# An AdaLN block with attention and a routed feed-forward: the near slots move in front of the last three dense tiles

## The reference, cut to what matters

```python
h = _layernorm(x) * (1 + ca) + sa
x = x + ga * attention(h)              # 16 heads of 128, causal, 1024 tokens
h = _layernorm(x) * (1 + cb) + sb
logits = h @ gate_w.T                  # 8 experts
top_vals, top_idx = top_k(logits, 2)
w = softmax(top_vals)
y = einsum('td,eod->teo', h, expert_w) + expert_b
x = x + gb * sum(take(y, top_idx) * w)
```

## Time and profile before

| | |
|---|---|
| times of 3 executions | 896.4, 898.64, 899.07 us |
| the profiled execution | 900.1 us, its span 898.2 us |
| PE busy | 867.4 us (97%) |
| DVE busy | 743.5 us (83%) |
| ACT busy | 541.2 us (60%) |
| POOL busy | 325.6 us (36%) |
| DMA | 43.08 MB, mean 48 GB/s |

### The profile page before, as it was taken

How to read it: one execution, slowest core, us unless ns; L and a number is a source line. 1 busy time by engine, 2 the same in 40 slices (tenths; PEclk the granted TensorE clock), 3 DMA queues, 4 the chain that set the end, 5 groups by cost and what they waited for, 6 DMA issues and landing times.

```text
span 898.2 us, 16979 instructions
## 1 busy us (share of the span) xinstructions
PE 867.4 (97%) x5399; PEld 771.4 (86%) x5399; DVE 743.5 (83%) x1688; ACT 541.2 (60%) x1247; POOL 325.6 (36%) x398
## 2 busy tenths in 40 slices
PE   6999999999999999999999999999999999999985
PEld 5778888888888888888888889988998888889884
DVE  6687888888888888878878888888889989887666
ACT  4477666666666666664566666666666656664351
POOL 4454222222222222231534444444422224576644
PEclk9999999999999999999999999999999999999998
DMA  7000620000000000200000000000000000352563
GB/s 246 7 12 12 229 65 14 12 12 12 12 12 12 12 12 12 96 17 7 1 24 13 14 12 13 13 12 14 12 13 13 13 12 30 130 171 77 195 210 112
DMA packets 36649, 43.08 MB, mean 48 GB/s; under 512 B 3060, under 2 KB 33814, under 8 KB 36502
## 3 DMA queue, kind: packets, MB, share of 16 engines
q1 hardware_dynamic: 34216, 35.94, 12.4%
q0 software_dynamic: 2304, 6.29, 2.2%
q10 hardware_dynamic: 64, 0.02, 0.0%
HBM read 32.02 MB, written 15.20 MB: 53 GB/s over the span
## 4 chain that ended last, share of the span: by engine, by line
PE 89%; DVE 5%; ACT 2%; DMA 1%; issue 1%; POOL 0%; SPq 0%; DVEq 0%; ACTq 0%
PE ps_t L1063 13%; PE ps_s L952 9%; PE ps_s L956 9%; PE ps_s L953 9%; PE ps_o L944 7%; PE ps_o L948 7%; PE ps_o L945 7%; PE ps_m L952 3%; PE ps_m L956 3%; PE ps_m L953 3%; PE ps_m L944 3%; PE ps_m L948 3%; PE ps_m L945 3%; PE ps_o L1073 1%; PE ps_t L1152 1%
## 5 line engine op out<-in xcount | busy, mean ns | idle before, releaser
L1423 ACT ACTIVATE pt_hi<-ps_t 128x512 fp32r<-128x512 f32 (+2 forms) x320 | 170.9, 534 | 124.6 <-PE ps_t L1063 124.2
L1473 ACT ACTIVATE probs<-ps_s,neg_max 128x128 f32<-128x128 f32 (+7 forms) x256 | 189.9, 742 | 79.5 <-DVE neg_max L1857 76.5
L1866 DVE TENSOR_TENSOR pt_lo<-ps_t,pt_hi 128x512 fp32r<-128x512 f32 (+2 forms) x320 | 192.1, 601 | 13.0 <-ACT pt_hi L1423 9.1
L1857 DVE TENSOR_REDUCE neg_max<-ps_s 128x1 f32<-128x128 f32 (+7 forms) x256 | 192.3, 751 | 3.7
L703 POOL TENSOR_TENSOR q_lo<-raw,q_hi 128x512 fp32r<-128x512 f32 x60 | 77.4, 1290 | 312.5 <-ACT q_hi L1423 312.4
L1063 PE MATMUL ps_t<-ident,probs 128*128 128x128 f32 x1152 | 188.6, 272 | 0.9 <-DVE pt_lo L1866 0.9
L1063 PEld LDWEIGHTS ps_t<-ident,probs 128*128 128x128 f32 x1152 | 141.8, 141 | 20.7 <-DVE pt_lo L1866 4.9
L952 PE MATMUL ps_s<-k_hi,q_hi 128*128 128x512 f32 (+2 forms) x354 | 148.5, 420 | 2.4 <-ACT probs L1473 2.4
L1904 DVE SCALAR_TENSOR_TENSOR acc<-ps_m,rsum,acc 128x256 f32<-128x256 f32 x256 | 111.3, 476 | 16.3 <-PE ps_m L956 15.7
L956 PE MATMUL ps_s<-k_hi,q_lo 128*128 128x512 f32 (+2 forms) x354 | 123.3, 348 | 0.0
L1851 DVE TENSOR_TENSOR ps_s<-ps_s,mask 128x128 f32<-128x128 f32 x256 | 75.4, 295 | 57.0 <-PE ps_s L956 49.5
(11 more groups left out here) (311 smaller groups left out, 1719.4 us busy)
## 6 DMA issues: line engine op xcount, KB each, us to landing
slot_out_dram<-y_slot SPq DMA_DIRECT2D x38, 128.0 KB, 1.7
wq_raw<-in_L_attn_wq_dram SPq DMA_DIRECT2D x32, 128.0 KB, 2.3
wo_raw<-in_L_attn_wo_dram SPq DMA_DIRECT2D x32, 128.0 KB, 2.0
wkv_raw<-in_L_attn_wkv_dram SPq DMA_DIRECT2D x2, 1024.0 KB, 6.3
acc<-in_L_attn_x_dram SPq DMA_DIRECT2D x2, 1024.0 KB, 15.4
we_raw<-in_L_ffn_expert_w_dram SPq DMA_DIRECT2D x1, 2048.0 KB, 8.4
slot_rows<-slot_rows_dram SPq DMA_DIRECT2D x2, 1024.0 KB, 7.6
slot_rows_dram<-in_L_attn_x_dram SPq DMA_DIRECT2D x1, 1920.0 KB, 16.4
```

The costliest lines, as they stand in the source:

```text
L1423: return nc.scalar.activation(dst, src, ACT.Copy, scale=scale)
L1473: nc.scalar.activation(probs[par][:, prob_offset(i):prob_offset(i) + w], ps_s[:, i % 2, col:col + w], ACT.Exp, bias=neg_max[:, par, i:i + ...
L1857: nc.vector.tensor_reduce(neg_max[:, par, i:i + 1], ps_s[:, i % 2, col:col + w], AXIS_X, ALU.max, negate=True).then_inc(max_set, 1)
L1866: nc.vector.tensor_tensor(pt_lo[:, q % PT, lo:CH], ps_t[:, q % 2, lo:CH], pt_hi[:, q % PT, lo:CH].bitcast(F32), ALU.subtract).then_inc(pt_ ...
```

## The change

The near slots stand directly behind dense tile 0; dense tiles 1 to 3 follow them. The transposes of the first two near slots, which lay behind the third and fourth expert pair of tile 1, now lie behind those of tile 0. Joins 0 to 5 lie among the near slots, joins 6 to 10 inside tiles 1 to 3, join 11 behind the last finish. SP issues the second and third load of near rows when the first has landed. The gates of the late rows, the reading of their logits and the work on them are one slot later each, and the low plane of slot 0 is made one step earlier on DVE.

```diff
-JOIN_AT = {1: 1, 3: 2, 6: 3, 9: 4, 12: 5}
+JOIN_AT = {2: 0, 5: 1, 7: 2, 9: 3, 11: 4, 13: 5}
+DENSE_EARLY = 0
@@ banks
-            return kv_bank(s % 2) if s < SLOTS else kv_bank(2 + (s - SLOTS) % 2)
+            return kv_bank(s % 2)
-            return kv_bank((e2 + (2 if d < 2 else 0)) % 4)
+            return kv_bank((e2 + 2) % 4)
@@ SP
             for i, (lo, hi) in enumerate(((0, 3), (3, 9), (9, SLOTS1))):
+                if i == 1:
+                    sp.wait_ge(slots1_in[0], 16)
                 sp.dma_start(slot_rows1[:, lo:hi, :], slot1_v[:, lo:hi, :]).then_inc(slots1_in[i], 16)
...
@@ PE
                 if s in (SLOTS, SLOTS + 1):
-                    pe.wait_ge(*((first_mixed, 4) if s == SLOTS else (mixed, LATER_MIXES + 2)))
+                    pe.wait_ge(mixed, LATER_MIXES)
-                elif d == 2:
-                    pe.wait_ge(*((mixed, LATER_MIXES + 4 + 2 * e2) if e2 < 2 else (slot_out, ALL_SLOTS)))
+                elif d == 1 and e2 in (0, 2):
+                    pe.wait_ge(*((first_mixed, 2) if e2 == 0 else (slot_out, ALL_SLOTS)))
-            gate_after = {4: 0, 5: 1, 7: 2, 9: 3, 12: 4, 14: 5, 16: 6, 18: 7}
+            gate_after = {4: 0, 5: 1, 7: 2, 9: 3, 13: 4, 15: 5, 17: 6, 19: 7}
             for d in range(HALF):
-                if d == 2:
-                    for s in range(SLOTS, ALL_SLOTS):
-                        if s + 2 < ALL_SLOTS:
-                            turn_slot(s + 2)
-                        slot_product(s, near_e[s - SLOTS])
                 for e2 in range(EXPERTS // 2):
+                    if d == 1 and e2 == DENSE_EARLY:
+                        for s in range(SLOTS, ALL_SLOTS):
+                            if s + 2 < ALL_SLOTS:
+                                turn_slot(s + 2)
+                            slot_product(s, near_e[s - SLOTS])
                     experts(d, e2)
-                    if d == 1 and e2 == 0:
+                    if d == 0 and e2 == 1:
                         pe.wait_ge(n_place_set, 1)
                         near_e.extend(chosen(n_expert_u, SLOTS1))
-                    if d == 1 and e2 >= 2:
+                    if d == 0 and e2 >= 2:
                         turn_slot(SLOTS + e2 - 2)
@@ DVE, behind the slots of batch 0
+            mix(0, {})
+            slot_lower(SLOTS)
+            slot_lower(SLOTS + 1)
+            finish(0)
+            hidden2_lo(2)
+            for s in range(SLOTS, ALL_SLOTS):
+                if s + 2 < ALL_SLOTS:
+                    slot_lower(s + 2)
+                if s - SLOTS in JOIN_AT:
+                    join(JOIN_AT[s - SLOTS])
+            mix(1, {5: 6})
+            hidden2_lo(3)
+            finish(1)
+            mix(2, {3: 7, 7: 8})
+            mix(3, {3: 9, 5: 10})
+            finish(3)
+            join(JOINS - 1)
```

More of the change, by code:

```diff
@@ L586, in _ @@
             store_mixed(0)
-            store_mixed(1)
-            store_joined(0)
             for s in range(SLOTS1):
@@ L592, in _ @@
                     store_joined(JOIN_AT[s - 1])
-            for j in range(NT - 2, NT + 2):
+            store_joined(6)
+            store_mixed(1)
+            for j in range(7, JOINS - 1):
                 store_joined(j)
+            store_mixed(2)
             store_mixed(3)
-            store_joined(NT + 2)
-            store_joined(NT + 3)
-            store_mixed(2)
+            store_joined(JOINS - 1)
             for i in range(2):
@@ L1703, in _ @@
                     hidden2_hi(s - 16)
-                if s == 19:
+                if s == 20:
                     read_logits(late, 2 * HALF)
-                if s == 21:
+                if s == 22:
                     gap_exponential(late)
             slot_finish(SLOTS - 1)
[L1709 to L1714, removed]
-                            slot_finish(s - 1)
-                        if s - SLOTS in JOIN_AT:
-                            weigh_first(JOIN_AT[s - SLOTS])
-                    slot_finish(ALL_SLOTS - 1)
-                mix_first(d)
-                if d == 1:
-                    slot_upper(SLOTS)
-                    slot_upper(SLOTS + 1)
-                if d + 2 < HALF:
-                    hidden2_hi(d + 2)
-                if d == 1:
-                    weigh_first(0)
-                if d == 2:
-                    weigh_first(NT - 2)
-                    weigh_first(NT - 1)
-            for j in range(NT, JOINS):
+            mix_first(0)
+            slot_upper(SLOTS)
+            slot_upper(SLOTS + 1)
+            hidden2_hi(2)
+            for s in range(SLOTS, ALL_SLOTS):
+                if s + 2 < ALL_SLOTS:
+                    slot_upper(s + 2)
+                if s > SLOTS:
+                    slot_finish(s - 1)
+                if s - SLOTS in JOIN_AT:
+                    weigh_first(JOIN_AT[s - SLOTS])
+            slot_finish(ALL_SLOTS - 1)
+            mix_first(1)
+            weigh_first(6)
+            hidden2_hi(3)
+            mix_first(2)
+            weigh_first(7)
+            weigh_first(8)
+            mix_first(3)
+            for j in range(NT + 1, JOINS):
                 weigh_first(j)
@@ L1957, in frame @@
                     if q == 11 and not nxt:
+                        if b + 1 == B:
+                            slot_lower(0)
                         add_projection(n, par, b, 0, 1)
@@ L2305, in finish, with mix @@
                                         ALU.add).then_inc(yout_set[par], 1)
-            def mix(d, joins):
+            def mix(d, joins, some=range(2, EXPERTS)):
                 par = d % 2
-                for e in range(2, EXPERTS):
+                for e in some:
                     if e % 2 == 0:
@@ L2321, in mix @@
                         join(joins[e])
-                    if d == 1 and e in (5, 6):
-                        slot_lower(SLOTS + e - 5)
             def join(j):
@@ L2341, in _ @@
             n = B * HEADS - 1
-            slot_lower(0)
             slot_lower(1)
```

25 lines of the change are left out of this document (5 added, 20 removed).

## The result

Median of 11 executions: 901.63 us (900.32 to 904.03) against 899.07 us (896.4 to 901.33) of the kernel before in 11 executions beside it. The forecast was 0.7 us more (899.3 us), in a range of 895.3 to 902.8 that held the time.

A forecast was written before the change was run, and what follows sets the result against it. PE stalls and low clock in the near slots, then DVE at the end, were taken as the bound. Last matmul 890.8 plus 8.1 gives 898.9 against 898.2; 0.7 on the 898.64 median gives 899.3 us, range 895.3 to 902.8.

The forecast's parts named there:

- mixes and low plane on DVE: Behind the fourth pair of tile 0: DVE mixes two halves (0.87 us), then makes the first near slot's plane (0.42).
- first two slots: Behind the stall: 2.5 us of DVE planes and tile 0's finish cover these slots; the third slot starts at 857.0.
- the gates: Late-row gates one slot later: PE's 0.66 us wait for DVE goes; 0.3 us taken, between 0 and 0.7.
- The wait for the load: Before the first near slot's transposes: PE stands 4.4 us, until the near rows land at 849.4.
- The load alone: First near-row load, issued without the other two: little won, landing in 3.4 us, between 2.5 and 3.9.
- The clock: Behind the stall: 1.2 GHz for two transposes and the fourth pair; full clock 1.8 us less, slow slots 1 more.
- The slots: The thirteen slots left: 13.9 us, plus 0.7 (0 to 2.5) for slack eaten at joins and a late store.
- The end: Behind the last matmul: 8.1 us in place of 10.1, 2.0 us won; bounds 6.6 and 8.7.
- A: Faster rival at the first-load wait: the stall costs only its length, 2.4 GHz kept; 897.0 us; chance 0.20.
- B: Slower rival at the fourth near slot: the second load comes late, PE stops again; 901.8 us; chance 0.18.
- C: Rival in slots and load: DVE falls behind, the load gains nothing alone; 1.2 us more, 900.5; chance 0.12.
- The signs: Idle 4.4 us, clock 0.50, second stop over 1 us, last matmul 2 to 3 us later, end some 8 behind.

The follow-up runs named there:

- gates_only: The kernel before with only the gates of the late rows and their ACT and DVE steps one slot later; no difference that can be told.
- unsplit: The changed kernel without SP's wait between the first and second load of near rows; the same time as the changed kernel within its interval.
- warm: The changed kernel with 19 unread matmuls filling PE's wait for the first load; ratio 1.0001 to the kernel before, 2.0 us back from the change.
- early_rows: The changed kernel, its first near-row load taken from batch 0's buffer without waiting for the scatter; 1.9 us faster than the changed kernel.
- two_pairs: The changed kernel with near slots behind tile 1's second pair, their first two transposes behind its first and second; 897.29 us, ratio 0.9982 to the kernel before.
- warm_join4: The changed kernel with 19 filler matmuls in the wait and four joined buffers in place of two; ratio 0.0005 below that of warm.
- join4: The changed kernel with four buffers for joined tiles in place of two; ratio 0.0006 (0.5 us) lower than the change, not distinguishable from nothing.

## Why the prediction was right, and by which steps

The number was right by a range that is wide for this change, and in part because errors of opposite sign met. Counted from the issue of the first load, which the forecast had at 846.04 and the trace has at 845.72:

```
step                                    forecast   trace    difference
landing of the first load               3.4        3.69     +0.3
transposes and fourth pair              3.6        3.69     +0.1
mixes and low plane on DVE              1.5        1.28     -0.2
first two slots                         2.5        3.75     +1.3
thirteen slots                          14.6       15.31    +0.7
dense tiles 1 to 3                      19.2       19.06    -0.1
from there to the end                   8.1        7.20     -0.9
sum                                     52.9       54.0     +1.1
```

From the same point to the end the kernel before takes 51.86 us, so the forecast had 1.0 us more here and 0.3 us less ahead of it, from the gates; that is its 0.7. The trace has 2.1 us more here. Ahead of it nothing was won: gates_only shows the wait moved, and that the load is issued 0.6 us earlier than before is no gain of the edit, since this execution lacks the low clock at 29 to 34 us. Of the traces that have that stretch, the four of changed kernels issue the load at 846.7 to 846.9, and the kernel before at 846.34.

**The wait for the load: right.** 4.51 us for 4.4, released by the load.

**The load alone: right.** I took little gain from it and put it at 3.4 us between 2.5 and 3.9; it took 3.69, and 3.6 with the others behind it. The low bound of 2.5, worked out from a bandwidth, was reached in no trace (3.4 to 4.0).

**The clock: right in kind, too small in size.** The granted clock fell to 0.50 and the pair took what was forecast. I let it recover at the pair's end and kept "low for the first two slots too, 1 us more" as the upper bound. That bound is what happened in the profiled execution, where the clock was back just before 858; in unsplit's trace it returned sooner, and the same stretch took 1.5 us less. In the place of this cost the forecast had DVE's queue: finish and planes were to delay the third slot to 857.0. In the trace DVE waited for PE's transposes by way of ACT instead, 0.81 us at 857.45. This is the mis-sized term, +1.3 us in this execution, and warm put the clock's whole price at 2.7 us in its trace and 2.0 us in time, where the forecast held 1.8. The mean clocks, 0.9915 over the changed kernel's executions and 0.9935 over those of the kernel before, point the same way, but they count stretches in which nothing is lost and cannot be turned into the price of this one.

The Trainium skill (TensorE: Matmul & The Clock Gate, section "HAM oscillation — how this bites in real kernels") says that a matmul burst behind a long DMA wait starts cold. The changed kernel and early_rows agree (clock 0.50 behind 4.51 and 2.45 us); behind the shorter waits for loads in two_pairs (1.08 and 1.85 us) the clock is 1.00; and warm shows the reverse: with the wait filled the clock stays at 1.00.

**The slots: half right.** PE stood for 0.76 us here, for 0.7 forecast, but by another cause: five joins were cheap, as assumed, and one was held 1.0 us by its buffer, not by a slowly eaten slack. The late store that I took over from the kernel before did not occur in this trace; unsplit and warm have it. The 0.7 us more are in the slots themselves: PE was busy for 14.55 us in place of 13.9, and from transposes to transposes a slot took 1.13 us on average, without the stall, and not 1.10.

**The end: right in sign, 0.9 us too cautious.** DVE ended 4.9 us past the last matmul and not 5.4, and the last store took 2.3 and not 2.7. Of the 5.4, 0.2 were a slip: 8.4 less 3.2 is 5.2. The slowed DVE step beside POOL's finish is there (0.84 at 887.50) and lies ahead of the last matmul, as the forecast had it.

**Rivals.** A fell: the clock did drop. B did not occur, but its mechanism is real and showed itself in four kernels in which PE came to the fourth slot sooner (0.19 us in warm, 0.22 in warm_join4, 1.85 in two_pairs, 2.45 in early_rows). C was right about the load and wrong about DVE.

**The signs.** The wait, the clock behind it and an end more than 7 us behind the last matmul came as said. The second stop was 0.87 us and not over a microsecond, and the last matmul ended at 892.5, 4.4 us later than 888.1 and not 2 to 3.

The forecast was 1.4 us below the measured difference (0.7 against 2.1, interval 1.2 to 3.0). 1.1 of this are the terms above, with the clock as the largest and the end as a credit against it; the other 0.3 are the gates.

## What to carry to other kernels

Before work that waits for a transfer is moved forward, compare when its data can land with when the engine would come for it, and put as much independent work of the same engine in front of it as the difference: here two expert pairs (with the loads issued at once) turned +0.23% into -0.32%. A stall of PE is priced at its length plus what the low clock takes behind it, until the clock is seen to be back and not until the next step ends. And once such a stall goes, look at the next load and the buffers of the stores: the next waits in these traces stand there. Before two traces are compared, look at the clock over the whole of each: here a low stretch 800 us ahead of the change goes with a shift of about a microsecond in everything behind it.

## What the runs showed of the hardware

- **How long PE stood, and what the clock did.** In the traces from 840 us on, stalls of 1.04 to 1.85 us (eight kernels) left the granted clock at 1.00; stalls of 2.19 (gates_only), 2.22 (before), 2.45 (early_rows) and 4.3 to 4.5 us (after, unsplit, join4) came with 0.50. These are single traces: the executions of two_pairs, with its 1.85 us, have mean clocks from 0.999 (896.4 us) down to 0.992 (901.95 us), and what lowered the clock in the slow ones is not shown.
- **The clock falls inside a long stall, or just behind one of 2.2 us.** In before PE was back at work at 858.75 and the clock fell at about 859.2; in gates_only it was 857.46 and about 857.8. In the longer stalls it fell while PE stood. In after it was 0.85 over the microsecond from 847 and 0.50 from 848, while the rows landed at 849.4; in join4, with a stall as long, it fell only at 849.4, and in unsplit already at 846.5. Where it fell earlier it also came back earlier: at 853.2 in unsplit, 857.9 in after and 859.6 in join4. Why it stays low for about 7 us in one and 10 in the others is open.
- **The spread between executions goes with the clock, and not only in this stretch.** In every kernel the time falls with the mean clock of its executions (correlation -0.44 to -0.99), by 0.5 to 0.8 us for 0.001 in most of them. Six of the twelve profiled executions have a clock of 0.50 for a while between 29 and 34 us, with PE at work: in before it follows sixteen matmuls of 2 columns each and a stall of 0.50 us at 27 us, and matmuls of 512 columns start 0.43 us apart in it and 0.23 us apart elsewhere. Where it is there, the first load is issued about a microsecond later.
- **The clock column does not hold at the start of a trace.** At 8.13 us in before, behind a stall of 5.54 us, those sixteen matmuls take 3.55 us against 1.95 at 27 us, with 1.00 in both windows.
- **Loads in one queue.** The first load of 384 KB landed in 3.4 to 4.0 us in all traces, alone or with 1.5 MB behind it. A load of 768 KB took 4.83 (warm) and 4.94 us (early_rows) in the chain of waits, while POOL's gathers ran beside it.
